# Graph attention and aggregation on one core: when the second pass issues its loads against the merged row's transposes, two low parts on VectorE one place earlier, and another order in the tail

## What is computed

```python
def attention(x):
    q, k, v = x @ Wq.T + bq, key @ Wk.T + bk, value @ Wv.T + bv
    s = (q @ k.T) / 4096 ** 0.5 * adj
    s = where(abs(s) < 1e-5, -1e9, s)
    return softmax(s) @ v @ Wm.T + bm
x = layernorm(x + attention(x))
x = layernorm(x + relu((adj @ x) @ W.T + b))
```

## Time and profile before

| what | value |
|---|---|
| median of 3 runs | 2011.98 us (2007.5 to 2013.18) |
| the profiled execution, its own time | 2021.37 us |
| its span, first to last instruction | 2019.6 us |
| PE busy | 1938.3 us (96%) |
| DVE, ACT, POOL busy | 1543.1, 872.1, 165.0 us |
| mean granted TensorE clock | 0.989 |
| DMA: software queue, hardware queue | 22.2%, 56.7% of 16 engines' span |
| second pass, from 744 us; tail, from 1538 us; last x1 row's product, 1627 us | |

### The profile page before, as it was taken

One profiled execution on the slowest core, in us unless ns is written; L12 is line 12 of the kernel. 1 busy time (PEld: TensorE's weight loads), 2 busy tenths in 40 slices (PEclk: granted clock), 3 DMA queues, 4 the chain that ended last, 5 costly groups with the idle time before them and its releaser, 6 DMA issues.

```text
span 2019.6 us, 26392 instructions
## 1 busy us (share of the span) xinstructions
PE 1938.3 (96%) x8859; PEld 878.7 (44%) x8859; DVE 1543.1 (76%) x3203; ACT 872.1 (43%) x1166; POOL 165.0 (8%) x262
## 2 busy tenths in 40 slices
PE   8988999999999999998999999999999799999998
PEld 5433444444444444443444444444444344444443
DVE  7898788888888846766777777777677337788887
ACT  5775555565666554544554555555454100000000
POOL 6000000000000020000000000001001000000000
PEclk9998999999999999999999999999999999999999
DMA  8657998899999897878778778777878987555551
GB/s 296 230 175 176 236 263 220 208 257 245 259 246 261 214 314 199 206 154 157 172 177 159 183 172 178 182 176 175 165 181 204 217 254 161 125 129 137 133 134 60
DMA packets 582118, 393.21 MB, mean 195 GB/s; under 512 B 479728, under 2 KB 506352, under 8 KB 580208
## 3 DMA queue, kind: packets, MB, share of 16 engines
q1 hardware_dynamic: 550624, 269.55, 56.7%
q0 software_dynamic: 31376, 122.17, 22.2%
HBM read 190.32 MB, written 117.44 MB: 152 GB/s over the span
## 4 chain that ended last, share of the span: by engine, by line
PE 71%; DVE 9%; DMA 8%; SPq 5%; ACT 3%; issue 3%; DVEq 0%; ACTq 0%
PE ps L1081 23%; PE ps L1060 22%; PE ps L1224 16%; DMA PT<-Phl 5%; PE ps L1094 3%; PE ps L1109 3%; SPq L458 2%; DMA UT<-Uhl 2%; PE ps L1013 2%; DVE prob L1982 1%; PE ps L1179 1%; ACT prob L1433 1%; DVE Phl L2010 1%; ACT Phl L1441 1%; SPq L605 1%
## 5 line engine op out<-in xcount | busy, mean ns | idle before, releaser
L1081 PE MATMUL ps<-V,PT 128*128 128x512 f16 x3072 | 704.1, 379 | 3.8 <-issue 3.7
L1060 PE MATMUL ps<-KG,left 128*128 128x512 f16 x2688 | 626.9, 382 | 28.4 <-ACT ps L1421 17.6
L1081 PEld LDWEIGHTS ps<-V,PT 128*128 128x128 f16 x3072 | 300.4, 98 | 367.7 <-issue 6.5
L1060 PEld LDWEIGHTS ps<-KG,left 128*128 128x128 f16 x2688 | 262.4, 98 | 355.7 <-issue 46.7
L1428 ACT ACTIVATE small<-prob 128x512 f32<-128x512 f32 x256 | 159.4, 628 | 266.9 <-DVE prob L1982 244.9
L2010 DVE SCALAR_TENSOR_TENSOR Phl<-prob,Phl 128x2048 f16<-128x2048 f32 x64 | 146.7, 2292 | 114.7 <-ACT Phl L1441 81.2
L1421 ACT ACTIVATE ps<-ps 128x512 f32<-128x512 f32 x192 | 111.4, 580 | 180.0 <-PE ps L1060 180.0
L1994 DVE CUSTOM_DVE_ANT_0 prob<-prob,small 128x512 f32<-128x512 f32 x256 | 173.7, 688 | 2.9
L1988 DVE TENSOR_SCALAR small<-small,eps_s,neg_s 128x512 f32<-128x512 f32 x256 | 136.8, 543 | 35.5 <-ACT small L1428 33.6
L1670 ACT ACTIVATE p<-ps 128x512 f32<-128x512 f32 x14 | 8.4, 597 | 348.0 <-PE ps L1224 348.0
L1441 ACT ACTIVATE Phl<-prob 128x2048 f16<-128x2048 f32 x64 | 121.9, 1904 | 53.8 <-DMA PT<-Phl 51.8
(11 more groups left out here) (225 smaller groups left out, 2020.6 us busy)
## 6 DMA issues: line engine op xcount, KB each, us to landing
adjh<-in_adj POOLq DMA_DIRECT2D x64, 512.0 KB, 8.3
adj_bf<-adjh SPq DMA_DIRECT2D x32, 512.0 KB, 6.8
adj_bf<-adjh POOLq DMA_DIRECT2D x32, 512.0 KB, 7.4
left_dram<-left SPq DMA_DIRECT2D x16, 896.0 KB, 5.9
xraw<-in_x_t SPq DMA_DIRECT2D x8, 1024.0 KB, 8.8
t_dram<-tq POOLq DMA_DIRECT2D x8, 1024.0 KB, 5.5
t<-t_dram SPq DMA_DIRECT2D x32, 256.0 KB, 7.8
x_in<-in_x SPq DMA_DIRECT2D x32, 256.0 KB, 3.2
```

Source lines behind the costliest of these rows:

```text
L1060: last = nc.tensor.matmul(ps[:, bank, :], left[:, s, k, d * P:(d + 1) * P], KG[gr][:, RIGHT[k], m, d, :], start=(first and n == 0), stop=( ...
L1081: last = nc.tensor.matmul(ps[:, BU + b, :], PT[:, b, s, m, :], V[:, v, m, :], start=(m == 0 and n == 0), stop=(m == MT - 1 and n == 2))
```

## The change

- SP, `second_period`: from i = 2 on, the late left factors and x of row 2i-3 are issued after the `UT` pair of row 2i-4, at the start of the period. Before, they were issued at the end of the period before, ahead of that pair. The late left factors of period 17 are still issued in period 16.
- POOL, `second_period`: from i = 2 on, the two adjacency loads wait until the `UT` pair of row 2i-4 has landed (`ul_in`).
- DVE: `y_low(2i-4)` stands ahead of `z_made(2i-3)`, and `merged_low(2i-2)` ahead of the masks of blocks C22 and C21.
- Tail, SP: x of row 29 is loaded behind `UT` of row 28; the `UT` pair of row 30 goes ahead of all adjacency parts; the `x1T` pair of row 30 and the `UT` pair of row 31 go ahead of the parts of tile (0, 1). All twelve parts of the tiles (0, 1), (1, 0), (1, 1) then stand in a row ahead of `x1T` of row 31.
- Tail, POOL: Y chunk 3 waits for `UT` of row 28 to land; chunk 5 waits for `UT` of row 30 and no longer for `x1T` of row 29, as chunk 6 still does.

```diff
                     if i >= 2:
                         turn_merged_high(2 * i - 4)
                         turn_merged_low(2 * i - 4)
+                        load_left(q, True)
+                        load_x_again(2 * i - 3)
...
-                    if q + 1 < 2 * NP:
+                    if i == 0:
                         load_left(q + 1, True)
-                    if i >= 1:
-                        load_x_again(2 * i - 1)
...
                 turn_merged_low(NT - 4)
+                load_x_again(NT - 3)
...
                 load_o(NT - 1)
+                turn_merged_high(NT - 2)
+                turn_merged_low(NT - 2)
                 for b in range(2):
                     sp.wait_ge(ab_st[b], 16 * NP)
                     sp.wait_ge(t_st[b], T_DONE + 16 * (NP // 2 + 1))
-                for part in range(2):
-                    adj_part(0, 0, part)
-                turn_merged_high(NT - 2)
-                turn_merged_low(NT - 2)
-                for part in range(2, PARTS):
+                for part in range(PARTS):
                     adj_part(0, 0, part)
                 load_x_again(NT - 1)
                 turn_x1_high(NT - 3)
                 turn_x1_low(NT - 3)
+                turn_x1_high(NT - 2)
+                turn_merged_high(NT - 1)
+                turn_merged_low(NT - 1)
+                turn_x1_low(NT - 2)
                 sp.wait_ge(ph_in, 32 * NT)
                 sp.wait_ge(pl_in, 32 * NT)
                 for part in range(PARTS):
                     adj_part(0, 1, part)
-                turn_x1_high(NT - 2)
-                turn_merged_high(NT - 1)
-                turn_merged_low(NT - 1)
-                turn_x1_low(NT - 2)
...
                 def second_period(q):
                     i = q - NP
+                    if i >= 2:
+                        pool.wait_ge(ul_in, 16 * (2 * i - 3))
                     if i >= 1:
                         for b in range(2):
                             load_adj(q, b)
...
+                pool.wait_ge(ul_in, 16 * (NT - TC + 1))
                 load_y(3)
...
                 load_y(4)
+                pool.wait_ge(ul_in, 16 * (NT - TC + 3))
+                load_y(5)
                 pool.wait_ge(x1t_in, 32 * (NT - 2))
-                for c in range(5, 7):
-                    load_y(c)
+                load_y(6)
...
                     if i >= 2:
+                        y_low(2 * i - 4)
                         z_made(2 * i - 3)
...
                         x1_low(2 * i - 3)
+                    if i >= 1:
+                        merged_low(2 * i - 2)
                     masked(q, 1, C22)
-                    if i >= 2:
-                        y_low(2 * i - 4)
...
-                    if i >= 1:
-                        merged_low(2 * i - 2)
                     threshold(q, 1, C21)
```

## The result

| | before | changed kernel |
|---|---|---|
| median | 2009.74 us (4 runs, 2007.48 to 2013.18) | 2049.08 us (4 runs, 2039.29 to 2051.32) |
| ratio, 95% interval | | 1.0185 [1.0146, 1.0224] |
| profiled execution, its span | 2021.37, 2019.6 us | 2047.08, 2045.3 us |

The forecast was no change (2011 us, range 1998 to 2022). The kernel became 1.85% slower, outside the range. "i" numbers the periods of the second pass, P1 is a period's first score product, "P1 + 5" is 5 us after it.

A forecast was written before the change was run, and what follows sets the result against it. PE, busy 96% of the span, was taken as the bound, so only its gaps could change. Terms -1 + 4 - 4 = -1 us on the median 2012.0 gave 2011 us, range 1998 to 2022.

The forecast's parts named there:

- Term A: Second pass, gaps before `project`: earlier `UT` pair removes 14.7 us, nearly all given back at `PT`; -1 us, bounds 0 and -14.7.
- The worked period: Period of the 6.27 us gap: without it the second group would start at 952.6, but `PT` holds it until 960.3.
- Term B: Second pass, adjacency loads issued 2.6 us later push the `PT` pair slightly in 13 periods; +4 us, bounds 0 and +13.
- I take 0.3, near the lower end: Cost per period of the later adjacency loads, in us, chosen from 0, 1.0 or 2.3.
- The bound of +13: Upper bound, in us, on the cost of the later adjacency loads over 13 periods of the second pass.
- Term C: Tail: gaps before `UT` users and row 30 go, one of some 7 us reappears before row 31; -4 us, bounds -9 and 0.
- the 4.5 us that the sum had taken back: Tail: part of the first gap's gain given back, because the next row's `PT` low part lands late.
- Rival 2: Slower: `PT` pair shares DMA engines with adjacency loads, then stores; 1.0 us in 13 periods, 2020 or 2024 us; chance 0.26.
- threshold of 0.3 us: Spare time before PE's second group in a period; a `PT` delay beyond it was to cost PE time.
- Rival 1: Faster: transposes get clear of the adjacency loads and `PT` is not pushed; 2002 us, 1997 to 2006; chance 0.28.
- Rival 3: DMA queues take turns of equal size: second pass unchanged, tail alone gives -4, 2008 us; chance 0.08.

## Why the prediction was wrong, point by point

- **Term A (gaps before `project`): mechanism right, size only partly.** `UT` lands 2.5 us after its issue, no gap stands before `project`, and the gain is given back at the `PT` pair. SP's order alone measured 1.0039 [1.0009, 1.0068], where A = -1 us would be 0.9995: given back in full and a little more, by some us that nothing in the term stood for. The worked period says the same: the term puts its second group at 960.3, the trace has it at 961.11, so all of the 8.5 us are given back. With DVE's moves, on which the term counted to get the low part out at once, it measured 0.9957 [0.9929, 0.9985], about -9 us.
- **Term B (the loads wait): the step that failed.** The delay of the loads and that their own user doesn't feel it came out as told (issued about 3.7 us after P1, "about 3.5" forecast). The size did not: +4 us forecast; the changed kernel is about 41 us slower than the same kernel without the wait (2049.08 against 2008.07 us). That is 2.7 us in the mean of the twelve periods, 32 of the 37.8 us between the two profiled spans. DVE's wait was to grow from 21.5 to about 27 us and grew to 50.3; the second group was to stay at 24.6 to 25.5 and came at 24.9 to 32.4. The failing step is "I take 0.3, near the lower end": it held that most of the delay would be absorbed among the `PT` transposes. In the mean 2.9 of 3.3 us went through to the landing of `PT` low, since the packets of the pair's high part do not start before the loads are nearly done, and then run beside the stores, the first of which keeps its date at P1 + 12.6. With the stores out of the way 1.5 us went through and the loss was gone. The reason given for the low value, that SP's issue of `PT` high is freed when `UT` leaves the queue, did not hold: that issue took 5.83 us, not less than 3.32. The bound of +13 was too low by the term's own numbers as well: its upper cost of 2.3 us a period, times 13, is 30.
- **Term C (tail): direction of each piece right, sum not.** Row 30's gap is gone and one stands before row 31's product, 9.60 us rather than 7. The twelve parts were estimated at 19.3 us and took 21.4. Two gaps stood before these, with slow matmuls behind. The one of 2.22 us is, with these, 3.9 us, about the 4.5 us that the sum had taken back. The one of 2.88 us, before row 29's product, is new and not in the sum: this row's `x1T` pair is issued right behind four adjacency parts. And the rest of the kernel behind row 31's product became 2.6 us longer. In the five kernels with this tail it is 394.2 to 394.8 us, in the seven profiles with the old one 390.9 to 393.6; nothing in the sum stood for that, and its cause was not looked into. The tail alone measured 0.9991 [0.9957, 1.0025], which is -2 us and holds both -4 and 0.
- **Rival 2 was the right mechanism at the wrong price.** It said that the pair shares the DMA engines "with the adjacency loads and then the adjacency stores", and its mark for DVE's wait (over 35 us) was passed. It was priced from the same step as Term B, 1.0 us a period, so it ended at 2020 to 2024 and not near 2049. Its threshold of 0.3 us was not where it decides: loads at P1 + 2.4, 1.5 us later than before, cost nothing, and `PT` low lands at 20.3 to 23.0 as without the wait (19.4 to 23.0). They are issued later but land hardly later, as the landings above show.
- **Rival 1** (`PT` gets clear of the loads, 1997 to 2006 us) did not happen; it is what the kernels with late stores did (2001.79 us with the loads still late). **Rival 3** had turns of equal size; the turns are equal in number (240 to 234) and unequal in length.
- **DVE's two moves** were put at nothing. Alone they measured 0.9965 [0.9927, 1.0004], perhaps the most useful part of the change; the interval just reaches 1.

## What to carry to other kernels

When a load is delayed, don't only ask whether its own user feels it: list every transfer that shares the engines until the next deadline, with its date and its bare duration (packets times their time, over 16 engines), and see which two now overlap. The cost of a late issue need not be a slope: here nothing at 1.9 us, and 2.7 us a period at 3.3. Look at the landings, not at the issues: they had moved by 0.8 and 3.3 us. A transfer that nobody waits for soon, as the adjacency stores, is a candidate to go behind the one that everybody waits for; here that took 0.45% off the kernel before, and with it the changed kernel went from 1.0185 to 0.9948.

## What the runs showed of the hardware

- The two queues took turns by packet (240 to 234, 237 to 252). A packet of the casting load holds an engine for 322 ns, one of the plain store for 159, one of a transpose for 18 to 31. In such turns the 234 transpose packets got 8.6 us of engine time beside 77.6 us of the loads.
- A transpose that was issued while the loads ran, with nothing else ahead of it in its queue, got no packet through for 3.3 to 4.6 us, in all twelve periods of the changed kernel (in the one shown 174 to 0 in 1364 to 1369, although SP had begun the issue at 1365.88).
- The end of a transpose can come well after its data. In the undisturbed period of before, the last packet of `PT` low ended at 1307.3 and the part landed at 1310.6, with the stores in between. For `PT` high in the period of i = 12 the distance was 3.9 us in the changed kernel (1373.6 to 1377.5) and 1.4 us where the stores were late (1337.7 to 1339.1). Over the twelve periods the two overlap: 1.2 to 3.9 us and 1.0 to 2.8 us.
- SP's issue of one transpose is no constant: 3.32 and 2.92 us for the `PT` pair in a quiet period, 5.83 and 5.28 when the loads and stores stand in the way.
